# A message-passing layer with 80 edge chunks: 16 of them gathered by DMA instead of 12, six spill levels turned through 16 places instead of seven through 8, and the gathers issued at a later, even spacing

## What is computed

```python
h_self   = x @ W_lin + b_lin
messages = x[dst] @ W_msg + b_msg
msg_sum  = segment_sum(messages, src);  counts = segment_sum(1, src)
h_agg    = msg_sum / max(counts, 1)
h        = relu(concat([h_self, h_agg], 1) @ W_upd + b_upd)
out      = layernorm(x + h)
```

## Time and profile before

| | us |
|---|---|
| median of 3 runs | 1657.13 (1656.5 to 1659.34) |
| the profiled execution's own time | 1663.77 |
| its span, first to last instruction | 1662.0 |
| preparation, up to PE's first gather of pass 0 | 577.1 |
| pass 0 (from first to first ScalarE copy) | 55.3 |
| passes 1 to 23, each | 42.3 |
| tail behind pass 24 | about 15 |

### The profile page before, as it was taken

How to read it: one execution, slowest core, us unless ns; L and a number is a source line. 1 busy time by engine, 2 the same in 40 slices (tenths; PEclk the granted TensorE clock), 3 DMA queues, 4 the chain that set the end, 5 groups by cost and what they waited for, 6 DMA issues and landing times.

```text
span 1662.0 us, 42934 instructions
## 1 busy us (share of the span) xinstructions
PE 1352.0 (81%) x16656; PEld 829.0 (50%) x16656; DVE 1131.1 (68%) x2880; ACT 783.1 (47%) x1128; POOL 474.1 (29%) x512
## 2 busy tenths in 40 slices
PE   2868757667766279999999999999999999999997
PEld 2858757667666134444444444444444444444443
DVE  7999899999999425555555555555555555555554
ACT  1222213100010136666666666666666666666664
POOL 1000000000000244444444444444444444444430
PEclk9777768655555579999999999999999999999998
DMA  6222222132000353443434444444444444444420
GB/s 89 84 84 99 72 76 88 55 111 62 4 1 1 121 147 100 118 118 117 119 118 119 119 117 120 119 117 119 119 119 119 118 118 118 119 119 118 120 51 11
DMA packets 119790, 160.60 MB, mean 97 GB/s; under 512 B 32099, under 2 KB 91552, under 8 KB 119516
## 3 DMA queue, kind: packets, MB, share of 16 engines
q1 hardware_dynamic: 95426, 110.08, 20.1%
q0 software_dynamic: 22880, 47.02, 12.8%
q10 hardware_dynamic: 1290, 0.78, 0.2%
HBM read 134.62 MB, written 23.21 MB: 95 GB/s over the span
## 4 chain that ended last, share of the span: by engine, by line
PE 55%; DVE 31%; ACT 7%; issue 6%; DMA 1%; DVEq 0%; ACTq 0%; SPq 0%
PE slot L1233 30%; PE acc L1247 16%; ACT big L539 7%; DVE big L777 5%; DVE big L757 5%; DVE big L782 3%; DVE big L788 3%; PE acc L1258 2%; PE slot L1283 2%; DVE big L815 2%; PE acc L1266 2%; DVE big L808 2%; DVE big L784 2%; PE slot L1274 1%; DVE big L814 1%
## 5 line engine op out<-in xcount | busy, mean ns | idle before, releaser
L539 ACT ACTIVATE big<-slot 128x768 bf16<-128x768 f32 x850 | 649.7, 810 | 405.7 <-PE slot L1233 359.9
L1233 PE MATMUL slot<-big 128*128 128x384 bf16 x2900 | 553.0, 329 | 67.2 <-ACT big L539 46.9
L1233 PEld LDWEIGHTS slot<-big 128*128 128x128 bf16 x2900 | 244.1, 98 | 353.6 <-issue 177.5
L625 POOL DMA_INDIRECT big<-x,dst_at x300 | 292.2, 974 | 288.9 <-PE acc L1247 173.6
L1247 PE MATMUL acc<-big 32*128 32x385 bf16 x6800 | 352.5, 325 | 0.0
L929 DVE TENSOR_TENSOR big<-col_lo,iota_lo 128x512 bf16<-128x512 f16 x425 | 179.6, 423 | 239.7 <-PE acc L1247 226.0
L629 POOL DMA_INDIRECT big<-x,sp_i x175 | 175.7, 1004 | 286.6 <-PE acc L1266 135.7
L919 DVE TENSOR_SCALAR big<-big,iota_k 128x512 bf16<-128x512 f16 x725 | 228.9, 351 | 23.4 <-PE slot L1233 12.0
L1143 PE MATMUL acc<-big 125*100 125x64 f16 x1600 | 132.7, 260 | 118.3 <-DVE big L815 118.3
L1247 PEld LDWEIGHTS acc<-big 32*128 32x128 bf16 x6800 | 141.0, 93 | 175.6 <-issue 101.3
L1143 PEld LDWEIGHTS acc<-big 125*100 125x100 f16 x1600 | 127.7, 185 | 125.8 <-DVE big L815 125.8
(11 more groups left out here) (151 smaller groups left out, 1141.9 us busy)
## 6 DMA issues: line engine op xcount, KB each, us to landing
big<-rows SPq DMA_DIRECT2D x25, 2176.0 KB
x<-big SPq DMA_DIRECT2D x19, 480.0 KB, 2.8
big<-x SPq DMA_DIRECT2D x32, 192.0 KB, 2.4
big<-in_x SPq DMA_DIRECT2D x24, 256.0 KB
big<-base SPq DMA_DIRECT2D x24, 256.0 KB
out<-big SPq DMA_DIRECT2D x24, 256.0 KB
big<-in_x SPq DMA_DIRECT2D x19, 320.0 KB, 3.5
base<-big SPq DMA_DIRECT2D x19, 320.0 KB, 2.2
```

Source lines behind the costliest of these rows:

```text
L539: act.activation(xg[n % NX][:, :, 0:F3], slot[z % 2][:, :, 0:F3], ACT.Copy).then_inc(s["xg_ready"], 1)
L625: pool.indirect_dma_start(out=xg_d[:, c, 0:F3], out_offset=None, in_=x3_dram, in_offset=bass.IndirectOffsetOnAxis(ap=dst_at[:, q, c:c + 1] ...
L1233: ins = nc.tensor.matmul(slot[z % 2][:, j, 0:F3], W[R_ % NW_][:, k, (c % 4) * P:(c % 4 + 1) * P], xwin[:, win_at(c) + k, :], start=k == 0, ...
```

## The change

1. `CP` goes from 68 to 64: chunks 64 to 67, the last group of three windows, are gathered by DMA. A pass has 16 runs instead of 17, and 8 pairs of chunks by DMA instead of 6.
2. `LEV` goes from 7 to 6, and the table of turns has 16 places at a step of 2 slots instead of 8 at a step of 4. It is made by one `iota` with a mask on DVE, instead of 15 `iota`s.
3. `L_sp`, the one-hot matrix of the spills, has two buffers.
4. The runs behind which pairs and spills are added are given by lists, and so are the runs in which DVE makes the matrices for the pairs.
5. A gather waits for 5 more aggregated pairs (`LAG`), and `GAP` is 32 over 22.

```diff
-    LEV = 7
-    ROTS = 8
+    LEV = 6
+    ROTS, STEP = 16, 2
...
-    CP = 68
+    CP = 64
...
-        L_sp = shaped(two.take(8 * P, bf16), "p (a n j) -> p a n j", a=4, j=2)
+        L_sp = [shaped(two.take(8 * P, bf16), "p (a n j) -> p a n j", a=4, j=2) for _ in range(2)]
...
-        ORDER = [7, 0, 8, 1, 15, 2, 9, 3, 10, 4, 11, 5, 16, 6, 12, 13, 14]
+        ORDER = [7, 0, 8, 1, 9, 2, 10, 3, 15, 4, 11, 5, 12, 6, 13, 14]
...
+        PAIR_RUNS, SPILL_RUNS = [3, 4, 6, 7, 9, 10, 12, 14], [2, 5, 8, 11, 13, 15]
...
         def dma_pair_of(r):
-            return (r - 3) // 2 if r % 2 and 3 <= r < 3 + 2 * ND else None
+            return PAIR_RUNS.index(r) if r in PAIR_RUNS else None
 
         def spill_of(r):
-            return r // 2 - 1 if r % 2 == 0 and 2 <= r < 2 + 2 * LEV else None
+            return SPILL_RUNS.index(r) if r in SPILL_RUNS else None
...
+        PAIR_NODES = [1, 4, 7, 10]
...
-        GAP = STEPS / len(GATHERS)
+        GAP, LAG = STEPS / len(GATHERS), 5
...
-            for o in range(ROTS):
-                r = (4 * o) % SL
-                if r:
-                    pool.iota(raw_rot[:, o, 0:r, :], [[1, r], [0, 2]], base=SL - r, channel_multiplier=0).then_inc(s["tables_set"], 1)
-                pool.iota(raw_rot[:, o, r:SL, :], [[1, SL - r], [0, 2]], base=0, channel_multiplier=0).then_inc(s["tables_set"], 1)
+            pool.iota(raw_rot[:, :, :, :], [[-STEP, ROTS], [1, SL], [0, 2]], base=SL, channel_multiplier=0).then_inc(s["tables_set"], 1)
...
-                            pool.wait_ge(s["aggregated"], (q - 1) * STEPS + int(GAP * i) + 1)
+                            pool.wait_ge(s["aggregated"], (q - 1) * STEPS + int(GAP * i) + 1 + LAG)
...
-            dve.wait_ge(s["tables_set"], 2 * ROTS - 1 + 4)
+            dve.wait_ge(s["tables_set"], 5)
+            n = mark(nc.vector.tensor_single_scalar(raw_rot[:, :, :, :], raw_rot[:, :, :, :], SL - 1, ALU.bitwise_and))
+            after(n)
...
-                    if q > 0:
-                        dve.wait_ge(s["spilled"], q * LEV)
+                    if q > 1:
+                        dve.wait_ge(s["spilled"], (q - 1) * LEV)
...
-                            if r % 4 == 1 and r < 2 * ND:
-                                hot_dma_nodes(q, r // 4)
+                            if r in PAIR_NODES:
+                                hot_dma_nodes(q, PAIR_NODES.index(r))
```

More of the change, by code:

```diff
@@ L253, in gnn_program @@
         TURN, UPDATE, ROOT, LAYER, NORM = 5, 8, 10, 9, 11
+        PAIR_RUNS, SPILL_RUNS = [3, 4, 6, 7, 9, 10, 12, 14], [2, 5, 8, 11, 13, 15]
+        assert len(PAIR_RUNS) == ND and len(SPILL_RUNS) == LEV
         def dma_pair_of(r):
-            return (r - 3) // 2 if r % 2 and 3 <= r < 3 + 2 * ND else None
+            return PAIR_RUNS.index(r) if r in PAIR_RUNS else None
         def spill_of(r):
-            return r // 2 - 1 if r % 2 == 0 and 2 <= r < 2 + 2 * LEV else None
+            return SPILL_RUNS.index(r) if r in SPILL_RUNS else None
+        PAIR_NODES = [1, 4, 7, 10]
         GATHERS = []
@@ L939, in hot_spills @@
                 def hot_spills(q):
-                    if q > 0:
-                        dve.wait_ge(s["spilled"], q * LEV)
+                    if q > 1:
+                        dve.wait_ge(s["spilled"], (q - 1) * LEV)
                     cols = sp_lo[:, q, :].rearrange("p (a j) -> p a j", j=2)
-                    nc.vector.tensor_tensor(L_sp, spread2(cols, P), tbl(iota_lo[:, :, :], 4), ALU.is_equal).then_inc(s["Lsp_ready"], 1)
+                    nc.vector.tensor_tensor(L_sp[q % 2], spread2(cols, P), tbl(iota_lo[:, :, :], 4), ALU.is_equal).then_inc(s["Lsp_ready"], 1)
                 def take_sums(q):
@@ L1265, in aggregate_spills @@
                         rows = slice(h * SL, (h + 1) * SL)
-                        ins = nc.tensor.matmul(acc[h][:, 0:F3 + 1], L_sp[rows, v // 2, :, v % 2], xg_sp[rows, v, 0:F3 + 1], start=False, stop=False)
+                        ins = nc.tensor.matmul(acc[h][:, 0:F3 + 1], L_sp[q % 2][rows, v // 2, :, v % 2], xg_sp[rows, v, 0:F3 + 1], start=False, stop=False)
                     ins.then_inc(s["spilled"], 1)
```

## The result

The changed kernel takes 1632.96 us (1631.0 to 1634.69) beside 1658.24 us for the kernel before: a ratio of 0.9847 [0.983, 0.9864], 25 us less. The prediction was 1572 us, 1544 to 1601. The direction was right, and the time lies 32 us outside the range.

The account below looks back on a forecast made before the run. PE was taken as the bound. Passes 1 to 23 gain 23 x (2.34 + 0.2 + 0.8) = 76.8 us, pass 24 2.5, pass 0 7.8, less 1.9 at the start: 85.2 off, so 1572 us, range 1544 to 1601.

Parts of the forecast that it names:

- What bounds the kernel: In the passes PE alone is near its limit: busy 38.9 of 42.32 us, its waits all for ACT.
- The work on PE: Each pass: a 3-window gather, one aggregate and one level go, two pairs come; 2.34 us gained.
- the update: PE's 0.20 us wait before `update` in each pass, covered by a longer gather; 0.2 us gained a pass.
- The gathers' delay: PE's excess waits in passes while POOL gathers, 1.8 us; 0.8 gained a pass, bounds -0.6 to 1.8.
- C: Passes: delay stays in full or grows with close gathers; gain -0.6 to 0.3 us a pass, 1584 to 1604; chance 0.26.
- B: Passes: delay vanishes, belonging to gathers that wait for `spilled` or `dma_added`; 4.3 us a pass, 1549 or 1544; chance 0.20.
- D: Passes: the gathers' queue becomes the bound, slower than before from 1.94 us a gather; chance 0.03.
- E: Passes: no change, PE waits for ACT in other places and the pass keeps its length; chance 0.02.
- Pass 0: First pass, 55.3 us: 7.8 us gained, from a vanished window wait, 2 us of stalls and 2.34 of PE work.
- The wait of the 3-window run: First pass: PE's 3.51 us wait for windows of chunks 60 and up, expected to go.
- The five stalls: First pass, 584.9 to 593.0: 6.6 us of PE stalls while SP's loads are under way; 2 us gained.
- The start: Preparation with a table of 1024 values: longer `iota`, cast and mask add 1.9 us, between 0 and 2.5.

Follow-up runs that it names:

- e10: Number not tied to a run in the text; by order probably the changed kernel with LAG = 0 on a quiet chip: 1537.62 us, 0.9521.
- e12: Number not tied to a run in the text; probably the changed kernel without gathers after pass 0 (1553.2 us, 0.9365) or with reordered groups (0.984).
- e17: Number not tied to a run in the text; by order probably the changed kernel with LAG = 11 instead of 5, quiet chip: 1538.53 us, 0.9513.

## Why the prediction was off

**What bounds the kernel: right.** PE is the bound on both kinds of chip, the clock stays at full in the passes, and nothing waits for DVE, ACT's total or the queue.

**The work on PE, 2.34 us a pass, and 0.2 for the update: right.** The quiet chip shows them alone, 40.51 to 37.85: 2.66. Of it 2.34 are the matmuls as summed, 0.25 is the `update`'s wait (5.8 us in 23 passes), and 0.07 stays. The aggregates' prices, read from start to start, held.

**The gathers' delay, +0.8 us a pass, bounds -0.6 to 1.8: the step that failed.** The mean pass of after is 41.28 us on the delaying chip (949.40 over 23) against 37.88 on the quiet one, and 37.88 on the delaying chips too once the indirect gathers are gone: they cost 3.4 us a pass. In before the two kinds of chip differ by 42.30 less 40.54, 1.8, which is the figure that the comparison with pass 24 had given; that reading was right. (Before without its gathers was not run on a delaying chip.) So the term was not +0.8 but -1.6, and 2.4 us in 23 passes are 55 us, nearly the whole miss. Two steps led to it. The places in runs 13 to 16 without a wait near them were taken as gathers that do no harm; they had only met no wait of PE in before, where 21% of the updates behind a gather by itself are late too, and the same kind of gather, set off by `aggregated`, delays copies all over after's passes (rows at 1018.11). And the lower bound allowed for one more wait of the size of those seen, although the change shortened what lies between two gathers of POOL, put six of them close together and took away the PE work that covers a late copy. Had I scaled the 1.8 us by what the change does to its cause, the bound would have been elsewhere: three more close gathers, six in all, double it, and that is a loss of 1.8, where 1.6 was measured.

**The rivals.** C, that the delay grows with close gathers, was the right one in its sign, and ended at 1604 us because of that bound. B fell in the form that I gave it: on the quiet chip all of after's gathers are set off by `aggregated` (L1249 is the only matmul that POOL waits for in 640 to 1560 us), as the lag was meant to do, and on the delaying one the delay is larger than ever. There the profile puts 50 of POOL's waits, 34.7 us, down to L1260 and L1268, so a late update of `dma_added` or `spilled` may hold back a gather now and then; but of the updates due within 1.5 us behind gathers set off by L1249, 44% are late. That such gathers cost more than others is still possible, by the 45 us that LAG = 0 adds. D fell: 22 gathers fit into 37.85 us without a wait of PE for one, 1.72 us apart, so a gather holds the queue for less than that. The estimate of 2.2 us by the Trainium skill (DMA: Bandwidth & Descriptors, section on the anatomy of one DMA on the GpSimd path) would be 49 us a pass if a DMA held its queue for all of it; this trace shows that it doesn't. E did not come: on the quiet chip the pass is 2.66 us shorter, all of PE's work, and the new waits for ACT on the delaying chip go with late updates.

**Pass 0, 7.8 us: too small, and wrong in one cause.** The wait of the 3-window run went. On the quiet chip it was 8.82 us instead of 3.51, and the stretch up to the turn of pass 1 gained 13.3:

```profile
595.57 4.00 PE L1233 MATMUL slot<-big 128*128 128x384 bf16 x12 [8.82 <-issue]
```

The five stalls I put down to SP's loads. They are the opening burst of gathers: they are gone with plain DMAs, and on the quiet chip, where SP loads the same. In after the burst has three more gathers and each stall comes again, about 0.9 us before each of a row of single matmuls:

```profile
585.76 0.48 PE L1235 MATMUL slot<-big 128*128 128x384 bf16 x1 [0.94 <-issue]
587.17 0.48 PE L1235 MATMUL slot<-big 128*128 128x384 bf16 x1 [0.93 <-issue]
588.58 0.48 PE L1235 MATMUL slot<-big 128*128 128x384 bf16 x1 [0.93 <-issue]
```

So this stretch gained 1.7 us where the burst delays.

**The start, -1.9 us: too much.** The `iota` took 2.82 us (estimate 3.0) and the mask 0.96 (1.0), but the cast of 1024 values took 0.69, as that of 512 had the earlier trace rows, and DVE's first reduction started at 7.73 instead of the 8.8 that I expected:

```profile
6.25 0.69 DVE L683 CAST big<-big 128x1024 f16<-128x1024 int32 x1
...
7.73 2.74 DVE L694 TENSOR_REDUCE low_f<-big 80x1 f32<-80x2500 int32 x1
```

On the quiet chip PE's flag matmul behind the preparation came 0.2 us later than before (564.23 and 564.00). That it came 4.6 us earlier in the profile of after (559.44) than in that of before (564.02) is luck and no part of the change: with the same preparation it came at 559.78, 562.15 and 564.68 in three other executions (e10, e12, e17). So the 5.8 us gained before PE's first gather in the comparison above are mostly not the change's.

**In sum.** On a quiet chip the change is worth 78.3 us of span: 1.25 before PE's first gather, 13.3 up to the turn of pass 1, 61.2 in the 23 passes and 2.55 behind. The forecast of 85.2 less the 18.4 for the gathers would have been 66.8. The 1538 us of the quiet chips lie outside the range as well, below it. On a delaying chip 37.6 of the 61.2 are taken back in the passes and 11.6 of the 13.3 ahead of them.

**What stays open.** What the indirect DMA does that a plain one doesn't; why four of the chips show nothing of it, and whether it is the chip at all or the time at which a comparison ran; and whether LAG = 5 helps because fewer gathers come close behind another, because none waits for its buffer, or because of where they fall. No version was found that beats the changed kernel on either kind of chip. With its gathers made harmless it would take 1538 us on both.

## What to carry to other kernels

Where the profile shows that something costs a little in the background (here 1.8 us a pass), don't count on a part of it as gain: work out what the change does to its cause, more of it and less cover, and let the lower bound go by that. A delay that is in no instruction's duration is found by setting the start of the reader against the start of the writer, with and without the suspect near. Measure on more than one chip before a figure of a few per cent is taken for the kernel's: here the same edit is worth 1.5% on one chip and 4.7% on another. And a lag that does nothing on one chip (1538 us with and without) can be 45 us on another.

## What was not expected of the hardware

- On three or four of the seven or eight chips an indirect DMA of 128 rows of 768 bytes, issued by GpSimd, makes the semaphore updates of PE's matmuls late: half of them by over 0.1 us in the changed kernel, 0.42 us in the mean. It costs 94 us of 1633, and 42 us of 1658 in the kernel before, there by the difference between the kinds of chip alone. On the other four there is none of it (at most 1.1% late).
- On the same chips plain DMAs of the same size from the same queue do nothing of the kind, nor does an `iota` of 0.41 us.
- The update of a matmul due within 1.5 us behind an indirect DMA that itself came close behind another was late in 93% of the cases (before) and 84% (after); over 1.75 us behind the last one, in 0 and 2%.
- During a burst of such gathers 1.25 us apart PE stalls before single matmuls for 0.9 to 2.0 us, without a releaser in the profile. 22 of them cost 15 us.
- DVE casts 128x1024 int32 to f16 in 0.69 us, the same as 128x512.
